# Sixteen expert units reordered by token halves, and the start of the second attention placed among them

## The reference, cut to what matters

```
x = x + L0_xattn(layernorm(x), ctx)   # 8 heads of 64
x = x + L0_ffn(layernorm(x))          # 8 experts, top 2
x = x + L1_xattn(layernorm(x), ctx)   # 16 heads of 8
x = x + L1_ffn(layernorm(x))          # +-1 weights: 256->512->512->128

def L0_ffn(x, Wg, W1, W2, W3):
    top_w, top_i = top_k(x @ Wg, 2); combine = softmax(top_w) at top_i
    h, g = x @ W1[e], x @ W2[e]       # for every expert e: 128 -> 256
    y = (silu(h) * g) @ W3[e]         # 256 -> 128
    return sum over e of y[e] * combine[:, e]

def L1_xattn(x, ctx, ...):
    q, k, v = x @ Wq + bq, ctx @ Wk + bk, ctx @ Wv + bv
    return softmax(q k^T / sqrt(8)) v @ Wo + bo     # per head, per batch

def layernorm(x): return (x - mean(x)) / sqrt(var(x) + 1e-5)
```

## Time and profile before

| what | us |
|---|---|
| three runs, lowest / median / highest | 233.52 / 233.78 / 233.90 |
| the profiled execution, its time | 234.19 |
| the profiled execution, its span | 232.1 |
| TensorE busy in the span | 223.3 (96%) |
| VectorE busy | 166.9 (72%) |
| ScalarE busy | 120.6 (52%) |
| GpSimd busy | 70.0 (30%) |

### The profile page before, as it was taken

One profiled execution on the slowest core, in us unless ns is written; L12 is line 12 of the kernel. 1 busy time (PEld: TensorE's weight loads), 2 busy tenths in 40 slices (PEclk: granted clock), 3 DMA queues, 4 the chain that ended last, 5 costly groups with the idle time before them and its releaser, 6 DMA issues.

```text
span 232.1 us, 5028 instructions
## 1 busy us (share of the span) xinstructions
PE 223.3 (96%) x1825; PEld 186.4 (80%) x1825; DVE 166.9 (72%) x433; ACT 120.6 (52%) x288; POOL 70.0 (30%) x105
## 2 busy tenths in 40 slices
PE   8999998899899999999999999999999999989994
PEld 8878887798886788988898889877688887766783
DVE  1677757898977795546555657988788788598862
ACT  2575948697853553223322334165655656757642
POOL 5624599124410305844042910342000000220200
PEclk9999999999999999999999999999999999999999
DMA  6970001000000002202202072000000000000003
GB/s 158 241 195 5 1 3 47 3 0 0 3 0 3 0 6 64 71 0 68 63 5 68 25 201 71 1 3 0 0 3 3 3 0 3 0 3 1 0 0 90
DMA packets 11868, 8.18 MB, mean 35 GB/s; under 512 B 3012, under 2 KB 11144, under 8 KB 11848
## 3 DMA queue, kind: packets, MB, share of 16 engines
q1 hardware_dynamic: 11848, 7.91, 12.7%
HBM read 5.81 MB, written 0.52 MB: 27 GB/s over the span
## 4 chain that ended last, share of the span: by engine, by line
PE 82%; ACT 8%; DVE 7%; issue 1%; POOL 0%; DVEq 0%; ACTq 0%; POOLq 0%
PE ps L676 12%; PE ps L478 9%; PE ps L850 9%; PE ps L480 9%; PE ps L479 9%; ACT probs L984 7%; PE ps L795 4%; PE ps L767 4%; PE ps L754 3%; PE ps L474 3%; PE ps L566 3%; PE ps L485 2%; PE ps L555 2%; PE ps L469 2%; DVE probs L1309 2%; PE ps L544 2%
## 5 line engine op out<-in xcount | busy, mean ns | idle before, releaser
L1041 ACT ACTIVATE kT<-ps 128x512 f32<-128x512 f32 x32 | 19.1, 598 | 47.2 <-PE ps L480 47.2
L676 PEld LDWEIGHTS ps<-w,kT 128*128 128x128 f32 x256 | 30.9, 192 | 1.2
L676 PE MATMUL ps<-w,kT 128*128 128x128 f32 x256 | 31.0, 275 | 0.0
L1385 DVE TENSOR_TENSOR kT<-ps,kT 128x512 f32<-128x512 f32 x32 | 21.8, 688 | 11.1 <-PE ps L480 8.8
L1392 DVE SCALAR_TENSOR_TENSOR x_sb<-ps,comb,x_sb 128x128 f32<-128x128 f32 x64 | 18.0, 342 | 13.5 <-PE ps L676 13.5
L478 PE MATMUL ps<-xT_hi,w_hi 128*128 128x512 f32 x64 | 26.7, 417 | 0.2 <-DVE kT L1385 0.2
L480 PE MATMUL ps<-xT_hi,w_lo 128*128 128x512 f32 x64 | 25.2, 393 | 0.0
L479 PE MATMUL ps<-xT_lo,w_hi 128*128 128x512 f32 x64 | 25.0, 390 | 0.0
L984 ACT ACTIVATE probs<-ps,negmax 128x128 f32<-128x128 f32 x64 | 22.6, 412 | 1.8 <-DVE negmax L1297 1.8
L1479 DVE TENSOR_REDUCE probs<-ps 128x8 f32<-128x1024 f32 x16 | 19.4, 1223 | 4.3 <-PE ps L754 4.3
L415 POOL TENSOR_TENSOR w_hi<-w_raw,zero 128x512 fp32r<-128x512 f32 x8 | 9.3, 1166 | 43.1 <-DMA w_raw<-in_L_ffn_W 28.4
(11 more groups left out here) (208 smaller groups left out, 511.1 us busy)
## 6 DMA issues: line engine op xcount, KB each, us to landing
w_raw<-in_L_ffn_W SPq DMA_DIRECT2D x16, 128.0 KB, 2.2
k_st<-h_a SPq DMA_DIRECT2D x12, 128.0 KB, 2.6
w<-in_L_ffn_W SPq DMA_DIRECT2D x8, 128.0 KB, 2.2
x_sb<-in_x SPq DMA_DIRECT2D x2, 256.0 KB, 5.1
ctx_sb<-in_ctx SPq DMA_DIRECT2D x2, 192.0 KB, 3.4
w_raw<-in_L_xattn_Wq SPq DMA_DIRECT2D x1, 256.0 KB, 5.1
wo<-in_L_xattn_Wo SPq DMA_DIRECT2D x1, 256.0 KB, 5.1
k_i<-in_L_ffn_k SPq DMA_DIRECT2D x1, 256.0 KB, 3.4
```

The source lines that it names most:

```text
L676: ins = pe.matmul(ps[:, 4 + slot, k * C:(k + 1) * C], uT[:, slot, c, k * P:(k + 1) * P], w3[:, buf, c, :], start=(c == 0), stop=(c == NH - 1))
L1041: act.activation(silu[:, c, :], ps[:, c, :], ACT.Silu).then_inc(b_silu, 1)
L1385: dve.tensor_tensor(uT[:, slot, c, :], ps[:, 2 + c, :], silu[:, c, :], ALU.mult).then_inc(b_u, 1)
```

## The change

The sixteen units become a table. `JOBS` lists eleven fetches of expert weights, `UNITS` the units as (job, half). Expert 0 runs on both halves, then experts 1 to 7 on half 0, then 7 down to 1 on half 1. Experts 7 to 4 are still held then, and experts 3, 2, 1 are fetched and split again (jobs 8 to 10). The weights stand in four slots instead of two. Slots 2 and 3 lie in tiles that are free in this stretch (`h_a`, `wo0`). The loops over experts become straight code. Half 0 is thus complete after the ninth unit (`LAST[0]` = 8), and its norm, its four queries, the first scores of batch 0 and the first maximum are written among the units of half 1. Half 1's root moves from GpSimd to VectorE. Six runs of filler (25) become four (`RAMP`, 14), and steps 0 and 1 are written out in another order.

```diff
...
+        RAMP = (5, 4, 2, 3)
...
+        JOBS = (0, 1, 2, 3, 4, 5, 6, 7, 3, 2, 1)
+        SLOT = (0, 1, 2, 3, 0, 1, 2, 3, 3, 2, 1)
+        UNITS = ((0, 0), (0, 1), (1, 0), (2, 0), (3, 0), (4, 0), (5, 0), (6, 0), (7, 0),
+                 (7, 1), (6, 1), (5, 1), (4, 1), (8, 1), (9, 1), (10, 1))
+        NU = len(UNITS)
+        LAST = tuple(max(q for q in range(NU) if UNITS[q][1] == t) for t in range(NT))
+
+        def done_before(j):
+
+            return max(q for q in range(NU) if UNITS[q][0] < j and SLOT[UNITS[q][0]] == SLOT[j]) + 1
+
+        def turn_of(j):
+
+            return sum(SLOT[i] == SLOT[j] for i in range(j + 1))
+
+        def added_before(q):
+
...
+        def up_hi(j):
+
+            s = SLOT[j]
+            return w12_hi[:, s, :] if s < 2 else h_a[:, 1, 2 * (s - 2), :]
...
+        def down_w(j):
+
+            s = SLOT[j]
+            return w3[:, s, :, :] if s < 2 else wo0[:, 2 * (s - 2):2 * (s - 2) + 2, :]
...
-        LN_BANK = ((M0, M0), (4, M0 + 1), (3, M0 + 1), (0, M0 + 1))
+        LN_BANK = ((M0, M0), (4, M0 + 1), (M0, M0 + 1), (0, M0 + 1))
...
-            return E_BANK if (b, a) == (0, 1) else S_BANK
+            return M0 if b == 0 else S_BANK
 
         def q_bank(n):
 
-            return n if n < NG else 5 + 2 * (n % 2)
+            return M0 + 1 - n % 2 if n < NG else 5 + 2 * (n % 2)
...
+            for j in range(2):
+                load_up(j)
+                load_down(j)
+            for j in (2, 3):
+                sp.wait_ge(b_lo, j - 1)
+                load_up(j)
+            sp.wait_ge(a_wo, NB)
+            for j in (2, 3):
+                load_down(j)
+            for j in range(4, len(JOBS)):
+                sp.wait_ge(b_lo, j - 1)
+                load_up(j)
+                sp.wait_ge(b_y, done_before(j))
+                load_down(j)
 
...
+            def split_up(j):
+                pool.wait_ge(ld_up[j % 2], 32 * (j // 2 + 1))
+                if j >= 4:
+                    pool.wait_ge(b_g, NH * done_before(j))
+                pool.tensor_tensor(up_hi(j), w12[:, j % 2, :], zero[:, :].to_broadcast([P, 2 * HID]), ALU.add).then_inc(b_hi, 1)
+                pool.wait_ge(b_hi, j + 1)
+                pool.tensor_tensor(up_lo(j), w12[:, j % 2, :], f32(up_hi(j)), ALU.subtract).then_inc(b_lo, 1)
...
+            pool.wait_ge(ln_lo, 2 * NT)
+            split_up(2)
+            split_up(3)
+            pool.wait_ge(b_acc, NT)
+            split_up(4)
             pool.wait_ge(masks, 6)
             pool.tensor_copy(k_st[:, :, :].rearrange("p g n -> p (g n)"),
                              is_lo[:, 1:2].to_broadcast([P, NG * NB * P])).then_inc(k1_fill, 1)
...
+            for j in range(8, len(JOBS)):
+                split_up(j)
             for b in range(NB):
-                if b == 4:
-                    ln_root(2, 1)
-
-                    pool.wait_ge(ln_rs, 3)
-                    chain(pool.tensor_tensor(nm[:, 4:NB], meanvar[:, 4:NB, 0], rs[:, 4:NB], ALU.mult))
-                    pool.tensor_scalar(nm[:, 4:NB], nm[:, 4:NB], -1.0, None, ALU.mult).then_inc(ln_nm, 1)
                 pool.wait_ge(ln_xn, 2 * NB + b + 1)
                 pool.tensor_tensor(x_sb[:, b, :], x_sb[:, b, :], bo1[:, :], ALU.add).then_inc(xb1, 1)
...
-            q = 2 * E - 4
-            b_down(q, 0, 0, NP - 1)
-            b_hidden(q + 2, 0, 1)
-            b_down(q + 1, 1, 1, NP - 1)
-            b_hidden(q + 3, 1, 1)
-            b_down(q + 2, 0, 0, NP - 1)
-            b_down(q + 3, 1, 1, NP - 1)
-            keep_busy(3, M0 + 1)
-            ln_transposes(2, 0)
-            keep_busy(7, M0)
-
...
-            for n in range(NG):
-                c_queries(n)
-            pe.wait_ge(k1_st, NK1)
-            keep_busy(6, M0)
...
+            for q in range(NU - 2):
+                b_down(q)
+                b_hidden(q + 2, (0,))
+                if q + 2 == LAST[0] + 4:
+                    ln_transposes(2, 0)
+                if q + 2 == NU - 3:
+                    c_queries(0)
+                elif q + 2 == NU - 2:
+                    c_queries(2)
+                elif q + 2 == NU - 1:
+                    pe.wait_ge(k1_st, NK1)
+                    c_scores(0, 0)
+                b_hidden(q + 2, (1,))
+                if q + 2 == NU - 3:
+                    c_queries(1)
+                elif q + 2 == NU - 2:
+                    c_queries(3)
+            b_down(NU - 2)
             c_scores(0, 1)
-            keep_busy(5, M0)
+            b_down(NU - 1)
             c_scores(1, 0)
+            pe.wait_ge(b_acc, NT + NU - 1)
+            c_turn_max(0)
+            keep_busy(RAMP[0], M0 + 1)
+            c_shifted(0, 0)
+            keep_busy(RAMP[1], M0 + 1)
+            c_shifted(0, 1)
+            c_values(0, 0)
+            keep_busy(RAMP[2], M0 + 1)
+            c_values(0, 1)
+            c_scores(1, 1)
             ln_transposes(2, 1)
-            keep_busy(2, M0)
-            c_turn_max(0)
-            keep_busy(2, M0)
-            c_scores(1, 1)
-            for s in range(NB + 2):
+            keep_busy(RAMP[3], W_BANK)
+            c_turn_max(1)
+            c_scores(2, 0)
+            c_shifted(1, 0)
+            c_queries(NG)
+            c_scores(2, 1)
+            c_queries(NG + 1)
+            c_shifted(1, 1)
+            c_turn_max(2)
+            c_queries(NG + 2)
+            c_scores(3, 0)
+            c_queries(NG + 3)
+            c_scores(3, 1)
+            c_values(1, 0)
+            c_tail(0, 0)
+            for s in range(2, NB + 2):
                 c_step(s)
 
             for n in range(4, len(D_ORDER) - 1):
@@ -1032,8 +1057,8 @@
 
             table(ACT.Silu)
 
...
+            for q in range(2, NU):
+                b_silu_step(q, (0,))
+                if q == LAST[0] + 4:
+                    ln_hi_copy(2, 0)
+                if NU - 3 <= q <= NU - 2:
+                    c_query_signed(2 * (q - NU + 3))
+                b_silu_step(q, (1,))
+                if q == LAST[0] + 3:
+                    ln_scale(2, 0)
+                if NU - 3 <= q <= NU - 2:
+                    c_query_signed(2 * (q - NU + 3) + 1)
+            table(ACT.Exp)
...
-            act.wait_ge(ln_nm, 1)
-            for b in range(4, NB):
-                act.activation(xn[:, b, :], x_sb[:, b, :], ACT.Identity, bias=nm[:, b:b + 1],
-                               scale=rs[:, b:b + 1]).then_inc(ln_xn, 1)
+            c_exp_half(0, 0)
+            c_exp_half(0, 1)
+            ln_scale(2, 1)
             ln_hi_copy(2, 1)
-            for s in range(NB + 1):
+            c_tail(0, 0)
+            c_exp_half(1, 0)
+            c_query_signed(NG)
+            c_query_signed(NG + 1)
+            c_exp_half(1, 1)
+            c_query_signed(NG + 2)
+            c_query_signed(NG + 3)
+            for s in range(2, NB + 1):
                 c_step(s)
...
+            for q in range(NU - 2):
+                unit_add(q)
+                if q == LAST[0]:
+                    unit_stats(0)
+                if q == LAST[0] + 1:
+                    ln_refine(0)
+                    ln_offset(0)
+                b_gate(q + 2, q % 2, (0,))
+                if q == LAST[0] + 2:
+                    ln_low(2, 0)
+                if NU - 3 <= q + 2 <= NU - 2:
+                    c_query_stack(2 * (q + 5 - NU))
+                b_gate(q + 2, q % 2, (1,))
+                if NU - 3 <= q + 2 <= NU - 2:
+                    c_query_stack(2 * (q + 5 - NU) + 1)
+                if q == LAST[0]:
+                    ln_seed_only(2, 0)
             dve.wait_ge(zeros_ok, 1)
             c_top(0, 0)
+            unit_add(NU - 2)
             c_top(0, 1)
+            unit_add(NU - 1)
+            c_shift(0)
+            unit_stats(1)
+            ln_seed_only(2, 1)
+            ln_refine(1)
+            ln_offset(1)
             c_top(1, 0)
-            c_shift(0)
+            c_top(1, 1)
+            c_shift(1)
             ln_low(2, 1)
-            c_top(1, 1)
-            for s in range(NB + 2):
+            c_top(2, 0)
+            c_query_stack(NG)
+            c_top(2, 1)
+            c_query_stack(NG + 1)
+            c_shift(2)
+            c_top(3, 0)
+            c_query_stack(NG + 2)
+            c_query_stack(NG + 3)
+            c_top(3, 1)
+            c_normalise(0)
```

194 lines of the change are left out of this document (56 added, 138 removed).

## The result

| what | before | after |
|---|---|---|
| seven executions each, median (us) | 233.54 | 234.67 |
| lowest / highest | 233.50 / 233.90 | 234.64 / 256.86 |
| ratio after / before | | 1.0053, 95% interval 1.0037 to 1.0068 |
| profiled execution, time / span | 234.19 / 232.1 | 235.94 / 234.1 |

The change makes the kernel slower by about 1.1 us (0.9 to 1.6 by the interval). The predicted time was 234.1, 0.3 above the kernel before, and the likeliest outcome was within 0.47 us of no change. That outcome didn't come. The range of 232.7 to 235.2 was wide enough to hold the result. One of the seven executions of the changed kernel took 256.86 us at a mean granted clock of 0.897. It is left out of the ratio, and it is the larger part of the story.

What follows compares the result with a forecast made beforehand. TensorE, busy 96%, was taken to set the end. Filler saving 2.58 us against waits costing 3.1 gave +0.47, taken as +0.3: 234.5 us profiled, 234.1 against the median of 233.78; eight-in-ten range 232.7 to 235.2.

Steps and rivals of the forecast that it cites:

- Units: Expert units up to the 15th down projection: queries, transposes and score group moved in cost 4.74 us, with no new wait.
- The hand-overs: From the 15th down projection to step 2 of the attention: 25.14 us, of which 4.08 waits and 14 fillers (3.28).
- The correction: Same stretch to step 2: the worked-forward +0.47 us lowered to +0.3, as the old order came out about 0.2 late.
- the prediction's own sign: Start of step 2 of the attention: before 172.0 means hand-overs over-costed, after 173.4 means under-costed.
- The pool from which a reordering can draw: Between the sixteenth expert unit and the second attention's steady state: 25 filler matmuls, 5.86 us, available to a reordering.
- Filler saves 2.58: From the 15th down projection to step 2: filler falls from 5.86 to 3.28 us, set against 3.1 of waits.
- rival (a): Hand-overs before step 2 shorter than taken, so filler savings come through: 231.5 to 233.3 us, centre 233.0; chance 0.31.
- The root: Half 1's root off GpSimd loses cover: 1.7 us now stand in VectorE's queue before both maxima of batch 1.
- Rival (b): VectorE becomes the bound from the last addition to step 2: 234.3 to 235.6 us, centre 234.9; chance 0.30 including late loads and clock.
- Rival (d): The clock falls in the new waits without filler, 0.5 to 0.9 us, before step 2; chance under 2%.
- The start of the units: VectorE's 0.88 us subtraction may take 0.2, but the gain ends at the next gate: 0, bounds 0.4 us either way.

Runs made afterwards that it cites:

- after_ref: The changed kernel run again unedited: 234.58 to 235.88 us in seven executions, 255.7 to 257.0 in five; ratio 1.0039 for those that kept the clock.
- before_half: The kernel before with 14 fillers instead of 25, in the old order: 233.24 against 233.84 us, ratio 0.9972, one execution of 263.5 in twelve.
- before_root: The kernel before with only half 1's root and offset moved from GpSimd to VectorE: 235.64 us in the one execution that kept its clock, others 238.8 to 269.0.
- after_poolroot: The changed kernel with half 1's root and offset back on GpSimd: 236.14 us in the one execution that kept its clock, others 240.9 to 263.9.
- after_slots: The changed kernel with weight slots 2 and 3 in `h_c` instead of `h_a`: 234.43 to 234.47 us where the clock was kept.
- after_score: The changed kernel with the first score group behind the last unit's second half, not between its halves: 234.32 to 234.38 and 235.56 us where the clock was kept.

## Why the prediction was right or wrong

**Units: mis-sized.** "TensorE is full there, so they cost what they cost behind it", 4.74 us. With the starts of the down projections in after_ref (147.91 - 78.40 = 69.51) against before (143.09 - 78.83 = 64.26), it is 5.25. Piece by piece: 1st to 3rd +0.11; 3rd to 11th 36.57 against 36.42, +0.15, the slots in `h_a`; 11th to 12th 5.02, where 4.55 + 0.59 was forecast, -0.12; two units with four queries 12.84, where 12.79 was; the last 5.35, where 4.55 + 0.45 was, +0.34. So the largest failing term is the score group, and the place of the weights was put at nothing. I took 0.45 us from the chain of waits, where the record of the group overlaps its neighbour. Standing alone it takes 0.59 start to start (151.31 to 151.90), and between the halves of a unit 0.79. That no new wait stands in the units was right: behind the third hidden part TensorE has none up to the 15th down projection, so the loads and splits came in time too.

**The hand-overs: right place, wrong sizes that cancelled by luck.** The longest waits stand on L784, L758 and L799 as said. They are shorter: 0.20 + 0.19 + 0.38 + 0.20 + 0.79 = 1.76 us, where 4.08 was forecast (those that the prediction lists sum to 3.95). The four of 0.15 to 0.35 between 154 and 162 are gone. The stretch takes 174.51 - 149.16 = 25.35 all the same, where 25.14 was forecast. The work between the waits is thus 20.3 us and not 17.8. Start to start, the 14 fillers take 4.20 us and not 3.28, which is 0.9 of the 2.5. The rest is as above: the same groups take longer where they stand apart. Seven score groups take 4.29 us, where eight took 4.11 before, the four transposed ones 2.41 (2.03 before) and the two down projections 3.93 (3.49 before). A ledger whose rest was called "waits" hid this: it gave the old order 1.0 us of them, where its trace shows 0.18.

**The correction: wrong.** Forward, the terms gave +0.47. I took 0.2 off because the old order came out 0.2 late. That error may have belonged to terms which the new order uses otherwise; no run shows it. Uncorrected, 0.47 with the 0.51 of the units and the 0.21 of the stretch behind them makes 1.19 us, against 1.23 at step 2. This only adds up the same readings and is no test of the terms. By the prediction's own sign (step 2 behind 173.4), 172.47 + 1.23 = 173.7 means terms that were too small.

**"The pool from which a reordering can draw": wrong.** The fillers stood mostly in what are else waits of the old order. Eleven fewer gave 0.6 us (before_half), and all 25 fewer lost the clock. "Filler saves 2.58" was therefore no saving to be had, and in rival (a) it was the main reason for 0.31.

**The root: true of the old order only.** "Taking GpSimd's root away is a loss of cover" holds there (before_root, +1.7). In the new order the same move is what keeps the scaled rows in time (after_poolroot, +1.5 when undone).

**Rival (a): didn't come.** The stretch it wanted shorter took 25.35 us, not less than the 25.14 forecast.

**Rival (b): the right side.** Its time of 234.3 to 235.6 held the result, but its mechanism isn't what happened. Half of the surplus lies in the units. At its two places the waits are 0.38 and 0.79 us, less than the 0.72 and 0.91 of my own sum. VectorE isn't busy throughout either, though TensorE's waits in this stretch all end on it: it waits for TensorE itself ahead of two of the six maxima between 159 us and step 2 (0.76 at 161.19, 0.83 at 170.61), and for ScalarE ahead of a stacking (0.87 at 166.46).

**Rival (d): wrong by far.** "The clock falls in the new waits", under 2%. It happened in 6 of 19 executions and cost 21 to 22 us each. The argument that "TensorE works between those waits" was no evidence. The change trades an execution that holds its clock for one that is at the edge.

**The start of the units: right.** The subtraction that took 0.88 us now takes 0.15, and the next hidden part waits for its gate, so the gain ends there:

```profile
80.30 0.15 DVE L1447 TENSOR_TENSOR gd<-top 128x8 f32<-128x8 f32 x1
```

```profile
86.49 0.47 PE L513 MATMUL ps<-xT_hi,h_a 128*128 128x512 f32 x1 [0.36 <-DVE kT L1416]
```

GpSimd's splits now run beside two other small steps, one with two inputs and a cast, and these are the slow ones in turn (0.34 and 0.51 before). The maxima of the ranking keep their 0.65 us. By the rule of the Trainium skill (GPSIMD Engine Reference, Specifications) that the prediction cites, they should; the maxima agree. The cast has one input, and no run shows in which mode it works.

```profile
76.04 1.26 DVE L1316 SCALAR_TENSOR_TENSOR bq_p<-bq,is_lo,bq_r 2x128 f32<-2x128 f32 x1
77.34 1.23 DVE L1319 CAST bq_s<-bq_p 2x384 fp32r<-2x384 f32 x1
```

What stays open: which activity gives the clock back once it is lost, why the same program loses it in one execution and not in the next, why after_slots and after_score lost it more often (16 of 25) than the changed kernel (6 of 19), and why weights in `h_a` cost 0.04 us per unit, save where queries stand in the unit.

## What to carry to other kernels

A matmul that computes nothing may be what holds TensorE's clock. Before counting it as a pool, take it out once and look at the granted clock over a dozen executions, since the median of five can hide a loss of 9% in every third. When a reordering leaves waits of TensorE in a row of them, put filler into each up to its length: here four cost nothing that could be measured, and the losses went from 22 of 44 in the three kernels without them to 0 of 18 in the two with them. Take a group's cost from start to start where it stands alone, not from a chain where records overlap.

## What was not expected of the hardware

- In the profiled execution of after_score the clock fell with TensorE busy for 4.62 and 4.01 us of two stretches of 5, and stayed at 1.2 GHz for about 50 us of work shown as unbroken. after_ref has the same busy times and kept it. The changed kernel lost it in six of nineteen executions, none of which was profiled.
- Twelve matmuls of 512 columns with weights in `h_a` take 0.04 us more per unit than with weights in `w12_hi` or `h_c` (4.59 against 4.55), in the six of eight units that hold no queries, and in the other two as well once the queries are taken out of them.
- A VectorE step of two rows (bias, 128 columns) took 1.26 us beside a GpSimd split, and a cast of 384 columns 1.23, where they had taken 0.34 and 0.51 before.
- TensorE reached its upper level at 8.1 us of the span in one execution of the changed kernel and at 12.4 in another. It shifts all that follows by 1.2 us, as much as the effect under study.
